# Four bank sums placed in front of two weight splits in VectorE's program, at the end of the cms stage

## The reference

```
q, k, v = x @ Wq, x @ Wk, x @ Wv
attn_out = softmax(q k^T * 512**-0.5) @ v @ Wp + bp
cms_out  = gelu(attn_out @ cW1 + cb1) @ cW2 + cb2 + one_hot(codes)      # hidden 2048
modifier = gelu(concat(attn_out, cms_out) @ mW1 + mb1) @ mW2 + mb2      # hidden 2048
y        = clip(x + cms_out + modifier, 0, 1)
h        = gelu(y @ W_down[role] + b_down[role])                        # 256 wide
out      = layernorm(y + h @ W_up[role] + b_up[role]) * gamma[role] + beta[role]
```

## Time and profile before

| what | us |
|---|---|
| median of three runs | 2097.38 (2095.5 to 2100.05) |
| the profiled execution's own time | 2097.53 |
| its span, first to last instruction | 2095.8 |
| TensorE (PE) busy | 2073.3 (99%) |
| VectorE (DVE) busy | 1588.5 (76%) |
| ScalarE (ACT) busy | 1097.1 (52%) |
| GpSimd (POOL) busy | 701.6 (33%) |
| DMA, mean over the span | 106 GB/s |

### The profile page before, as it was taken

One profiled execution on the slowest core, in us unless ns is written; L12 is line 12 of the kernel. 1 busy time (PEld: TensorE's weight loads), 2 busy tenths in 40 slices (PEclk: granted clock), 3 DMA queues, 4 the chain that ended last, 5 costly groups with the idle time before them and its releaser, 6 DMA issues.

```text
span 2095.8 us, 25018 instructions
## 1 busy us (share of the span) xinstructions
PE 2073.3 (99%) x9128; PEld 1701.9 (81%) x9128; DVE 1588.5 (76%) x1929; ACT 1097.1 (52%) x1625; POOL 701.6 (33%) x690
## 2 busy tenths in 40 slices
PE   9999999999999999999999999999999999999997
PEld 7887888888888888888888888888888888888884
DVE  4358878777868878867787887977686888787776
ACT  5366645454447654544454755544444666454444
POOL 1254415674002331766100332455400042165510
PEclk9999999999999999999999999999999999999999
DMA  8895444543212425444403222322130423421111
GB/s 304 239 236 143 133 114 120 130 119 101 103 46 105 154 76 138 114 113 103 129 30 133 88 71 83 99 61 61 45 127 0 151 74 104 115 61 59 52 61 41
DMA packets 183993, 221.94 MB, mean 106 GB/s; under 512 B 10288, under 2 KB 148272, under 8 KB 179776
## 3 DMA queue, kind: packets, MB, share of 16 engines
q1 hardware_dynamic: 175776, 184.58, 27.1%
q0 software_dynamic: 6720, 29.47, 7.8%
q10 hardware_dynamic: 1376, 6.29, 0.8%
HBM read 199.33 MB, written 62.91 MB: 125 GB/s over the span
## 4 chain that ended last, share of the span: by engine, by line
PE 93%; DVE 4%; ACT 1%; DMA 1%; issue 1%; SPq 0%; ACTq 0%; DVEq 0%
PE bank L864 30%; PE bank L866 30%; PE bank L865 30%; PE bank L919 1%; DMA stage<-ready_up 1%; DVE ring L1757 1%; DVE pc L2032 1%; PE bank L1262 1%; DVE xs L2207 0%; ACT ring L1298 0%; DMA fold_staging<-fold_w 0%; DVE ph_lo L2015 0%; PE bank L1233 0%; PE bank L1232 0%; PE bank L1231 0%
## 5 line engine op out<-in xcount | busy, mean ns | idle before, releaser
L1757 DVE TENSOR_TENSOR ring<-stage,ring 128x1024 fp32r<-128x1024 f32 (+1 forms) x288 | 356.1, 1246 | 67.2 <-ACT ring L1298 67.0
L864 PE MATMUL bank<-xa,ring 128*128 128x512 f32 x1016 | 396.1, 390 | 1.8 <-DVE raw_odd L1943 1.4
L866 PE MATMUL bank<-xa,ring 128*128 128x512 f32 x1016 | 395.3, 389 | 0.0
L865 PE MATMUL bank<-xa,ring 128*128 128x512 f32 x1016 | 395.3, 389 | 0.0
L864 PE MATMUL bank<-ph_hi,ring 128*128 128x512 f32 x808 | 317.1, 392 | 3.8 <-DVE pc L2032 1.8
L1298 ACT ACTIVATE ring<-stage 128x1024 fp32r<-128x1024 f32 (+1 forms) x288 | 271.8, 964 | 86.3 <-PE bank L866 40.2
L865 PE MATMUL bank<-ph_lo,ring 128*128 128x512 f32 x808 | 314.5, 389 | 0.0
L866 PE MATMUL bank<-ph_hi,ring 128*128 128x512 f32 x808 | 314.5, 389 | 0.0
L864 PE MATMUL bank<-vc,ring 128*128 128x512 f32 x672 | 261.7, 390 | 0.2
L866 PE MATMUL bank<-vc,ring 128*128 128x512 f32 x672 | 261.5, 389 | 0.0
L865 PE MATMUL bank<-vc,ring 128*128 128x512 f32 x672 | 261.4, 389 | 0.0
(11 more groups left out here) (202 smaller groups left out, 3698.6 us busy)
## 6 DMA issues: line engine op xcount, KB each, us to landing
stage<-ready_up SPq DMA_DIRECT2D x40, 896.0 KB, 5.2
stage<-mod_w SPq DMA_DIRECT2D x112, 256.0 KB, 3.4
stage_pair<-ready_pair SPq DMA_DIRECT2D x12, 1792.0 KB, 9.8
stage<-mod_w SPq DMA_DIRECT2D x28, 512.0 KB, 4.9
ready_up<-ready_up POOLq DMA_DIRECT2D x100, 128.0 KB, 5.1
ready_up<-cms_w SPq DMA_DIRECT2D x98, 128.0 KB, 3.4
ready_pair<-cms_w SPq DMA_DIRECT2D x42, 256.0 KB, 5.8
stage<-folded SPq DMA_DIRECT2D x16, 512.0 KB, 5.6
```

The source lines that it names most:

```text
L864: pe.matmul(dst, lh, rh, start=start and n == 0, stop=False, skip_group_check=not start)
L865: pe.matmul(dst, lh, rl, start=False, stop=False, skip_group_check=not start)
L866: done = pe.matmul(dst, ll, rh, start=False, stop=n == last, skip_group_check=not start)
L1757: dve.tensor_tensor(ring_part(key, 1), staged(key), f32(ring_part(key, 0)), ALU.subtract).then_inc(w_lo, 1)
```

## The change

The calls of the two splits move from the end of `cms_last` to a place in `cms_end` behind the loop over the four sums. `cms_end` follows `cms_last` directly, so this exchanges six neighbouring instructions of VectorE and nothing else, in each of the four rounds.

```diff
                 combine(r, n, C12)
                 hidden_lo(r, n, 2)
-                split_lo((r, "A", n + 1, 1))
-                split_lo((r, "C", n + 1, 1))
 
             def cms_end(r):
                 t0, step0, n = r * BUILDS, r * T_STEPS, CH - 1
                 for m in range(KT):
                     down_add(r, n, 0, m)
+                split_lo((r, "A", n + 1, 1))
+                split_lo((r, "C", n + 1, 1))
                 operand_lo(vc, B11, pc[:, 0, 0:2, :], cms_hi, t0 + 1, cms_lo)
```

## The result

The changed kernel takes 2103.15 us (median of 11 runs, 2101.95 to 2105.48) against 2098.18 of the kernel before in its 11 (2095.5 to 2100.05): ratio 1.0027, interval 1.0019 to 1.0035. It is slower by 5.0 us, where 2.0 us faster was forecast. The profiled spans say the same: 2101.6 against 2095.8.

What follows compares the result with a forecast made beforehand. TensorE (PE) was taken to bound the kernel, busy 2073.3 of 2095.8 us; closing its gap saves 4 x 0.50 = 2.0 us, late splits, loads and accumulates costing nothing: 2095.4 us against the 2097.38 median, range 2093.0 to 2099.6.

Steps and rivals of the forecast that it cites:

- The place of the gap and its price: PE's wait before the second-batch half of the down projection: 0.41 late start plus 0.09 slow start, 0.50 us a round.
- T4 in time: VectorE's T4 operand, released by the last accumulating transfer, had 2.0 us to spare before PE wants it; forecast cost nothing.
- I take x near 0: x is how much later the last accumulating transfer lands, bounded -1.1 to 3.0; cost max(0, x - 1.5) a round, taken as nothing.
- rival A: Stage loads late instead, queues sharing engines evenly: a load 1 us late costs at most 0.1 a round; 2095.8 us, 12%.
- B: Gain eaten by another wait at the same place, or by x about 2 us at T4: 2097.4 us, 15%.
- C: Traffic shifts whole, x = 3.0, PE waits at T4: 1.0 lost in two rounds, 0.7 in two; 2100.8 us, 9%.
- the same: Outcome within 0.2% (4.2 us) of the time before, neither under 2093.2 nor over 2101.6 us; given 0.91.
- four named cases: The forecast 60% (2095.4 us), late loads 12%, gain eaten 15%, slower by late T4 9%; 4% left for the unseen.

Runs made afterwards that it cites:

- e7: Changed kernel with SP's second and third load exchanged, weights C of slice 9 ahead of D of slice 8: 2095.87 us against 2096.89 before.
- e2: Kernel before with only the first of the four sums put in front of the two splits: 2094.58 us against 2097.23, ratio 0.9989.
- e1: Kernel before with only the split of weights C moved behind the four sums, split A staying in front: 2095.19 us against 2097.23, ratio 0.9989.
- e3: Kernel before, its order kept, with SP alone holding the first load until the fourth sum is counted: 2104.94 us against 2097.23, ratio 1.0035.
- e5: Changed kernel with POOL's first accumulating transfer held until the second split is done: 2102.62 us against 2096.89 before, ratio 1.0026.
- e6: Changed kernel with POOL's first accumulating transfer held until the third load has landed: 2119.58 us against 2096.89 before, ratio 1.0109.

## Why the prediction was wrong

**What held.** The place of the gap and its price: 0.50 a round was forecast and 0.51 measured. VectorE's new order, with 0.75 added to bring it on the axis of before: sums from 296.0 on (296.13 forecast), 0.60 of idle before the fourth (0.5), splits up to 300.9 (301.0), the operands 0.6 earlier than before (0.5). SP's first load 2.2 us later and POOL's accumulate 1.9 earlier in the trace, that is 3.0 and 1.2 on the common axis. T4 in time, which is the step "I take x near 0": it came out at -0.5 (317.31 + 0.75 against 318.56).

**The step that failed** is the sentence behind it: "The loads have more time to give: the first feeds a ScalarE split at about 313.8, the last one after 320". I costed the late loads at nothing, and in rival A at 0.1 a round, for a load that would be 1 us late. "After 320" says when the third load was wanted, and I never read when it landed: at 317.9. It had 2.9 us to spare, of which PE's gain takes 0.5, so a load 3.0 later had already used it up. It landed 4.1 later (321.27 + 0.75 against 317.9).

The row that carried the answer was among those quoted: the accumulate with 85% of the engines beside queued copies with 20%. I used it for the accumulate only, and misread its other half. The 20% were 426 packets with 0.40 MB, nearly 1 KB each; the copies' packets have 0.5 KB (318 to 319 in that trace, behind the loads' landing: 704 packets, 0.34 MB). So it was mostly the third load itself, at 0.06 MB per us, about a sixth of its pace alone. The accumulates' 2 MB take 12 us. In the changed kernel q1 had 9.2% at first and 27% over 304 to 317 as a whole, 1.12 MB, and with 0.64 MB moved before 304 some 1 MB of the loads was left behind 317. The first load was late too: ScalarE waited 1.45 us for it at 313.41, which VectorE and PE did not feel.

**The size.** Where the split of C was wanted: 321.87 before (the row is in the trace of before, with 0.34 of idle behind ScalarE), less 0.75 for the axis and 0.50 for PE's gain, is 320.62. It stood at 322.45: 1.83 late. The chain behind it on VectorE is closely packed, so all of that reached PE, in three portions: 0.34, 0.65 and 0.76 - 0.19 = 0.57 of longer steps, 1.56, and some 0.3 of slow starts. Each portion belongs to one waiting matmul, a door, and each door has less cover (time to spare before) than the one ahead of it. The first matmul on the new C weights (323.73) had 1.5 us of cover, for its split was done at 323.10 and it started at 324.65 before. The second (328.61) is the one that rival A looked at, with 0.6. The third had none: PE already waited there for a hidden part from VectorE. The profile calls this wait "issue", but PE starts 0.10 behind the end of that instruction in both traces (VectorE and PE before, then VectorE after; PE's row of after is shown above):

```profile
333.58 0.68 DVE L1954 SCALAR_TENSOR_TENSOR ph_lo<-raw,ph_hi 128x512 fp32r<-128x512 f32 x1
...
334.36 0.47 PE L864 MATMUL bank<-ph_hi,ring 128*128 128x512 f32 x1
...
334.18 0.68 DVE L1954 SCALAR_TENSOR_TENSOR ph_lo<-raw,ph_hi 128x512 fp32r<-128x512 f32 x1
```

Rival A took the cover of the second door for the whole road. A chain costs PE its lateness less the cover of the door that has least, and here that is nothing. 1.85 lost and 0.50 gained is 1.35 a round, 5.4 in all; the medians differ by 5.0, the spans by 5.8.

**The rivals.** A named the right transfer and the right engines and was given 12% and the wrong sign. Its price does not follow from its own rows either: 1 us late less 0.6 of cover is 0.4 and not 0.1 a round. B and C named the wrong transfer. Of the rule of the Trainium skill quoted there (DMA: Bandwidth & Descriptors, Queues, rings and completion order: round robin over the queues, packet by packet), the trace agrees that neither queue stands still for the other; I read it as an even share of time. By the rows of 304 to 308 the accumulate's 95 packets carried 0.78 MB, 8 KB each, the loads' 100 packets 0.10 MB, 1 KB each. The two queues took turns about evenly in packets as the trace counts them, and not in bytes or time.

**The chances.** 91% on "the same" rested on four named cases of which none let a load be more than 1 us late. The bound was there to be drawn: a third load that landed at 317.9 before, moved by the 3.0 of its issue, is 0.6 late against 320.3, at the least.

## What to carry to other kernels

A step that frees a buffer also sets when the next load starts: when it is moved, follow the load to its landing among everything else that the DMA engines carry then, and ask what each transfer's share is while the other is queued, not only who is issued first. Read first when that load lands now and when it is wanted: the difference is the whole allowance. Where transfers must be late, put the one wanted first ahead in the queue (e7), or move only as much as the wait needs: one sum of four (e2) or one split of two (e1) gave the whole gain and cost nothing. The gain here is 0.1% of the time; 0.5 us on the busiest engine is not worth 3 us on a queue whose slack has not been read.

## What the runs showed of the hardware

- Two queues with work at once took turns in packets: 95 packets of 8 KB against 100 of 1 KB in 4 us, so the load queue fell to 9% of the engines' time and a fourteenth of its own pace. From 311 to 312 in the same trace, where the accumulates' packets have 4 KB, it was 45 against 45, and 92% against 16%. Before, e1, e3 and e5 show the same pattern whenever both have work (83 to 92% for the accumulate in the 4 us behind its start).
- While loads are in flight, the accumulate's packets come long behind its issue: in the changed kernel it was issued at 299.10 and the stretch to 303.5 holds packets of q1 only. In e6, on free engines, 0.11 MB of it had moved between 312.70, its issue, and 314.3. Why the wait is some 3 us longer beside loads, though it was issued ahead of them, stays open.
- SP's third load took long to issue in the first round of the changed kernel and of e7 (three loads in 7.29 and 7.08 us instead of 1.60), not in e3 and e5. What holds the issue wasn't tried.
